# First two stacks of an attention kernel filled from tiles on chip, with the opening stage reordered

## The reference

```python
q, k, v = heads(x @ Wq + bq), heads(x @ Wk + bk), heads(x @ Wv + bv)      # x is layer-normalised
y  = softmax(causal(q @ k.T * scale)) @ v
qc, kc, vc = heads(x @ Wcq + bcq), heads(ctx @ Wck + bck), heads(ctx @ Wcv + bcv)
y += softmax(qc @ kc.T * scale) @ vc
x1 = x + (y @ Wp + bp)
z  = layernorm(x1); scores = (tanh(z @ gate_w.T) + 1) / 2
vals, idx = top_k(scores.T, 512)             # 4096 tokens, 8 experts
out = x1 + z.at[idx].add(expert_ffn(layernorm(z[idx])) * vals)
```

## Time and profile before

| | |
|---|---|
| median of three runs | 1717.27 us (1709.55 to 1719.33) |
| the profiled execution | 1720.7 us, of which the span is 1718.9 us |
| PE busy in the span | 1523.8 us (89%), mean granted clock 0.934 |
| DVE, ACT, POOL busy | 1176.9, 920.3, 427.0 us |

### The profile page before, as it was taken

The page is one execution under the profiler, slowest core; times in us unless marked ns, Lnnn a source line. Parts: engine busy times, 40 slices in busy tenths (PEclk is TensorE's granted clock), DMA queues, the critical chain, the costliest instruction groups (busy, mean ns, idle before and its releaser), DMA issues. The chain is left out here.

```text
span 1718.9 us, 26455 instructions
## 1 busy us (share of the span) xinstructions
PE 1523.8 (89%) x8913; PEld 719.2 (42%) x8913; DVE 1176.9 (68%) x3228; ACT 920.3 (54%) x1882; POOL 427.0 (25%) x863
## 2 busy tenths in 40 slices
PE   4469999999999999999999999999999624999997
PEld 3133344344434444443444344344433412566564
DVE  3367888788788778877887888787882156555441
ACT  2006777766677676777677677767767300211111
POOL 5002113132113213221321133131213301343332
PEclk9559999999999899999999999999999855999998
DMA  4981575285546727652855567185500120344332
GB/s 141 154 118 39 95 129 77 77 120 107 100 90 121 113 78 105 123 98 82 113 112 107 95 117 120 57 121 97 85 2 3 38 78 13 86 109 114 99 94 51
DMA packets 83467, 158.08 MB, mean 92 GB/s; under 512 B 12708, under 2 KB 46116, under 8 KB 83332
## 3 DMA queue, kind: packets, MB, share of 16 engines
q1 hardware_dynamic: 77188, 147.87, 44.8%
q0 software_dynamic: 6144, 8.52, 2.8%
HBM read 100.45 MB, written 55.71 MB: 91 GB/s over the span
## 5 line engine op out<-in xcount | busy, mean ns | idle before, releaser
L743 ACT ACTIVATE probs<-bank_ps 128x512 f32<-128x512 f32 (+3 forms) x1536 | 743.1, 545 | 297.6 <-PE bank_ps L541 291.9
L828 DVE TENSOR_REDUCE chunk_max<-bank_ps 128x1 f32<-128x512 f32 x1024 | 647.2, 682 | 112.3 <-PE bank_ps L572 109.8
L572 PE MATMUL bank_ps<-k_stack,q_stack 62*128 62x512 f32 (+3 forms) x1536 | 563.5, 446 | 32.5 <-DMA k_stack<-parts_dram 24.5
L541 PE MATMUL bank_ps<-q_stack,k_stack 64*128 64x512 f32 (+3 forms) x1536 | 545.5, 435 | 46.1 <-ACT probs L743 26.8
L572 PEld LDWEIGHTS bank_ps<-k_stack,q_stack 62*128 62x128 f32 x1536 | 256.0, 192 | 417.9 <-DVE chunk_max L828 180.3
L541 PEld LDWEIGHTS bank_ps<-q_stack,k_stack 64*128 64x128 f32 x1536 | 238.3, 188 | 133.2 <-ACT probs L743 103.9
L557 PE MATMUL out_ps<-probs,v_cross 128*32 128x512 f32 x2048 | 275.4, 610 | 0.0
L831 DVE CUSTOM_DVE_ANT_0 masked<-bank_ps,causal 128x128 bf16<-128x128 f32 (+3 forms) x512 | 232.3, 485 | 31.9 <-PE bank_ps L572 28.9
L986 POOL TENSOR_TENSOR pool_idle<-pool_idle 128x1 f32<-128x1 f32 x288 | 55.6, 193 | 627.9 <-ACT probs L743 429.5
L1263 ACT ACTIVATE h<-h_ps,b1T 128x512 f32<-128x512 f32 x64 | 44.0, 687 | 266.9 <-PE h_ps L1216 155.6
L887 DVE SCALAR_TENSOR_TENSOR parts<-bank_ps,bias,parts 128x512 fp32r<-128x512 f32 x80 | 60.0, 750 | 109.4 <-ACT parts L781 109.1
(11 more groups left out here) (147 smaller groups left out, 1313.5 us busy)
## 6 DMA issues: line engine op xcount, KB each, us to landing
parts_dram<-parts SPq DMA_DIRECT2D x80, 512.0 KB, 2.7
k_stack<-parts_dram SPq DMA_DIRECT2D x192, 192.0 KB, 11.7
q_stack<-parts_dram SPq DMA_DIRECT2D x192, 128.0 KB, 10.6
w1T<-in_L_ffn_fc1s SPq DMA_DIRECT2D x8, 1024.0 KB, 5.5
w2T<-in_L_ffn_fc2s SPq DMA_DIRECT2D x8, 1024.0 KB, 7.4
...
```

The costliest lines, as they stand in the source:

```text
L541: pe.matmul(bank_of(turn)[:, q0:T], k_stack[base:base + SIDE, g, pair, kc:kc + P], q_stack[base:base + SIDE, g, pair, qc + q0:qc + T], sta ...
L572: return pe.matmul(bank[:, 0:n], q_stack[base:base + MAX_ROWS, g, pair, qc:qc + P], k_stack[base:base + MAX_ROWS, g, pair, k0:k0 + n], sta ...
L743: nc.scalar.activation(probs[:, i % 2 * 2 + p, side, q0:T], bank_of(("score", g, i, p, side))[:, q0:T], ACT.Exp, scale=SCALE)\
L828: nc.vector.tensor_reduce(dst, bank[:, 0:n], AX.X, ALU.max).then_inc(max_done, 1)
```

## The change

- **Fills.** The stacks of units 0 and 1 are no longer read back from DRAM: `fill_directly` copies 16 rows of `parts` into 16 rows of a stack by DMA, one head at a time, so 24 DMAs a unit and half the size each. All 12 query copies of unit 0 go first, after qc is done; the 12 key copies after kc1; unit 1 follows. The first 24 maxima wait for one pair of heads (`first_in[0]`), the next 24 for the other, unit 1's for `second_in`.
- **Pieces.** The five pieces of half 1 move ahead of the value pieces and all maxima, and go to `probs` and `u_sb`, free at this time; their stores to DRAM follow the direct fills on SP. The three value pieces of half 0 run beside the maxima; those of half 1 move into the first batch, at (0, 1), (0, 4) and (0, 5), as in every other batch.
- **Opening.** Loads are split into what the first projections need (8) and the rest (7), with the context between them; x of sequence 1 is loaded after the first shift. DVE clears a quarter of `q_stack`, takes the statistics, and normalises x itself; POOL clears a quarter of `k_stack` first, makes the deviation, and clears the rest and the value tiles after it. Four matmuls on `ones_row` (`WARM_UP`) come first on PE.
- **Waits.** `fill` waits for one half fewer; ACT waits for the stores of half 1 before the first batch.

The core of the diff:

```diff
         return not (first and g == 0)
-    if name in LATER or (name in V_PIECES and half == 1):
+    if name in LATER:
         return not first
+    if name in V_PIECES and half == 1:
+        return True
...
-PROLOGUE = (("y0T0", 0), ("y0T1", 0), *((n, 0) for n in HALF_PIECES),
-            *((n, 0) for n in V_PIECES),
-            *((n, 1) for n in V_PIECES), *((n, 1) for n in HALF_PIECES), ("shift", 0))
-ALONE = PROLOGUE.index(("qc", 1))
+PROLOGUE = (("y0T0", 0), ("y0T1", 0), *((n, 0) for n in HALF_PIECES), *((n, 1) for n in HALF_PIECES),
+            *((n, 0) for n in V_PIECES), ("shift", 0))
+ALONE = PROLOGUE.index(("v", 0))
 UNWEIGHTED = 2
+WARM_UP = 4
...
+        def parts_of(piece):
...
+            if piece.of == 0 and piece.half == 1:
+                n = HALF_PIECES.index(piece.name)
+                return probs[:, n].bitcast(F32R) if n < 4 else u_sb[:].bitcast(F32R)
+            a, e = COL[piece.name]
+            return parts[:, :, a:e]
...
             def load_weights():
-                for name, tile in (("Wq", w_q), ("Wcq", w_cq), ("Wk", w_k), ("Wv", w_v), ("Wp", w_p)):
+                for name, tile in (("Wq", w_q), ("Wcq", w_cq), ("Wk", w_k)):
                     sp.dma_start(tile[:], w[name].rearrange("(t p) c -> p t c", p=P)).then_inc(weights_in, 16)
-                for name, tile in (("Wck", w_ck), ("Wcv", w_cv)):
-                    sp.dma_start(tile[:], w[name]).then_inc(weights_in, 16)
+                sp.dma_start(w_ck[:], w["Wck"]).then_inc(weights_in, 16)
...
                                  allow_slow_non_contiguous=True).then_inc(weights_in, 16)
...
+            def load_rest():
+                for name, tile in (("Wv", w_v), ("Wp", w_p)):
+                    sp.dma_start(tile[:], w[name].rearrange("(t p) c -> p t c", p=P)).then_inc(rest_in, 16)
+                sp.dma_start(w_cv[:], w["Wcv"]).then_inc(rest_in, 16)
...
                     sp.dma_start(bias_v[:, n, :], w[name].rearrange("(t p) -> p t", p=P),
-                                 allow_slow_non_contiguous=True).then_inc(weights_in, 16)
+                                 allow_slow_non_contiguous=True).then_inc(rest_in, 16)
                 sp.dma_start(bias_p[:], w["bp"].rearrange("(o c) -> o c", o=1).broadcast_to([P, C]))\
-                    .then_inc(weights_in, 16)
-                sp.dma_start(gateT[:], w["gate_w"].rearrange("p (t e) -> p t e", t=KT)).then_inc(weights_in, 16)
+                    .then_inc(rest_in, 16)
+                sp.dma_start(gateT[:], w["gate_w"].rearrange("p (t e) -> p t e", t=KT)).then_inc(rest_in, 16)
...
                 sp.wait_ge(*freed(piece))
-                if stacked is not None and name == HALF_PIECES[0]:
+                if stacked and name == HALF_PIECES[0]:
...
                         sp.wait_ge(slot_in[slot], stacked)
-                sp.dma_start(parts_dram[hf, :, :, a:e].rearrange("t c n -> c t n"), parts[:, :, a:e].bitcast(F32))\
+                sp.dma_start(parts_dram[hf, :, :, a:e].rearrange("t c n -> c t n"), parts_of(piece).bitcast(F32))\
...
                 hf, at = slot // 2, slot % 2 * UH * D
-                sp.wait_ge(parts_out, PARTS * halves)
+                sp.wait_ge(parts_out, PARTS * (halves - 1))
...
+            def fill_directly(slot, pair, of_q, landed):
...
+                a, e = (0, Q_COLS) if of_q else (Q_COLS, Q_COLS + K_COLS)
+                stack = q_stack if of_q else k_stack
+                for r, part in enumerate(Q_PART if of_q else K_PART):
+                    for side in range(SIDES):
+                        at = D * (UH * slot + SIDES * pair + side)
+                        to = SIDE * side + D * r
+                        sp.dma_start(stack[to:to + D, slot, pair].bitcast(F32), parts[at:at + D, part, a:e].bitcast(F32))\
+                            .then_inc(landed, 16)
...
                     for name in names:
-                        store_parts(find_piece(b, first, last, name, hf), FILL * b + FILL)
+                        store_parts(find_piece(b, first, last, name, hf), FILL * (b + hf))
...
                 if not last:
-                    sp.wait_ge(*freed(find_piece(b, first, last, "vc1", 1) if not first
-                                      else prologue_piece(PROLOGUE.index(("kc1", 1)))))
+                    sp.wait_ge(*freed(find_piece(b, first, last, "vc1", 1)))
...
             load_tokens(0)
+            load_weights()
             load_context(0)
-            load_weights()
-            sp.wait_ge(*freed(prologue_piece(PROLOGUE.index(("y0T1", 0)))))
-            load_tokens(1)
-            sp.wait_ge(stacks_clear, 2)
+            load_rest()
+            sp.wait_ge(q_clear, 3)
+            sp.wait_ge(k_clear, 2)
+            sp.wait_ge(*freed(prologue_piece(PROLOGUE.index(("qc", 0)))))
+            for pair in range(UH // SIDES):
+                fill_directly(0, pair, True, first_in[pair])
+            sp.wait_ge(*freed(prologue_piece(PROLOGUE.index(("kc1", 0)))))
+            for pair in range(UH // SIDES):
+                fill_directly(0, pair, False, first_in[pair])
+            for pair in range(UH // SIDES):
+                fill_directly(1, pair, True, second_in)
+                fill_directly(1, pair, False, second_in)
+            for name in HALF_PIECES:
+                store_parts(prologue_piece(PROLOGUE.index((name, 1))))
...
                                  [SHIFT_ROWS, UNITS * UH // SIDES * K_COLS // T, T])).then_inc(ones_in, 16)
-            for hf in range(2):
-                for name in HALF_PIECES:
-                    store_parts(prologue_piece(PROLOGUE.index((name, hf))))
-                fill(2 * hf, hf + 1)
-                fill(2 * hf + 1, hf + 1)
             put_shift(0, 0)
+            sp.wait_ge(*freed(prologue_piece(PROLOGUE.index(("y0T1", 0)))))
+            load_tokens(1)
+            fill(2, 2)
+            fill(3, 2)
...
                 kind, h, qt, chunk = MAX_ORDER[a]
-                if a == 0:
-                    pe.wait_ge(slot_in[g], FILL * b + FILL)
+                if b == 0 and g == 0:
+                    if a % (N_A // 2) == 0:
+                        pe.wait_ge(first_in[a // (N_A // 2)], DIRECT)
+                elif b == 0 and g == 1:
+                    if a == 0:
+                        pe.wait_ge(second_in, DIRECT * UH // SIDES)
+                elif a == 0:
+                    pe.wait_ge(slot_in[g], FILL * (b + g // 2))
...
-            def prologue_freed():
-                pe.wait_ge(*freed(prologue_piece(PROLOGUE.index(("vc1", 1)))))
-                pe.wait_ge(*freed(prologue_piece(max(n for n in range(len(PROLOGUE) - 1) if n < ALONE
-                                                     and PROLOGUE[n][0] in COL))))
...
+            pe.wait_ge(ones_set, 1)
+            for n in range(WARM_UP):
+                pe.matmul(bank_ps[:, BANKS - 1], ones_row[:, 0:P], ones_row[:], start=True, stop=True)
...
                 piece(prologue_piece(n), prologue_bank(n))
-            prologue_freed()
+            pe.wait_ge(rest_in, REST)
+            pe.wait_ge(*freed(prologue_piece(ALONE - 1)))
...
                 elif name in COL:
-                    a, e = COL[name]
                     halves = 2 * piece.of + hf
-                    if halves > 0:
-                        act.wait_ge(parts_out, PARTS * halves)
-                    nc.scalar.activation(parts[:, 0, a:e], bank[:], ACT.Identity,
+                    if halves > 2:
+                        act.wait_ge(parts_out, PARTS * (halves - 1))
+                    nc.scalar.activation(parts_of(piece)[:, 0], bank[:], ACT.Identity,
...
                 if n == UNWEIGHTED:
+                    act.wait_ge(weights_in, LOADS)
+                elif n == ALONE:
...
                 piece(prologue_piece(n), prologue_bank(n))
+            act.wait_ge(parts_out, PARTS)
...
-            nc.vector.memset(q_stack[:].bitcast(F32), 0.0).then_inc(stacks_clear, 1)
+            nc.vector.memset(ones_row[:], 1.0).then_inc(ones_set, 1)
+            nc.vector.memset(q_stack[:, 0].bitcast(F32), 0.0).then_inc(q_clear, 1)
...
             norm_stats(0, lambda t: x_sb[:, t, :], 1)
...
-            nc.vector.memset(ones_row[:], 1.0).then_inc(ones_set, 1)
+            nc.vector.memset(q_stack[:, 1].bitcast(F32), 0.0).then_inc(q_clear, 1)
+            dve.wait_ge(rstd_step[0], 2)
+            for t in range(NT):
+                nz = nc.vector.tensor_scalar(x_sb[:, t, :], x_sb[:, t, :], mean_var[:, 0, t, 0:1], rstd[:, 0, t:t + 1],
+                                             ALU.subtract, ALU.mult)
+            nz.then_inc(ln_done[0], 1)
+            nc.vector.memset(q_stack[:, 2:4].bitcast(F32), 0.0).then_inc(q_clear, 1)
             dve.wait_ge(weights_in, LOADS)
-            nc.vector.tensor_tensor(bias_v[:, 2, :], bias_v[:, 0, :], bias_v[:, 1, :], ALU.add).then_inc(v_bias_done, 1)
...
                 piece(prologue_piece(n), prologue_bank(n))
+            dve.wait_ge(rest_in, REST)
```

(6 more changed lines are left out.)

19 lines of the change are left out of this document (11 added, 8 removed).

## The result

The changed kernel takes 1689.24 us in the median of 4 runs (1687.51 to 1691.11), beside 1715.92 us (1709.55 to 1719.33) for the kernel before on the same chip: a ratio of 0.985, with 0.982 to 0.988 as its 95% interval. Timed a second time beside the experiments it took 1686.03 us (1684.95 to 1687.08), beside 1720.54: 0.981 (0.978 to 0.984). So it is faster by 1.5 to 1.9%. The prediction was 1687, with a range of 1671 to 1700. The medians lie 26.7 us apart, the two profiled executions that the stages are read from 33.2 us (1720.7 and 1687.5): of the four timed executions of the changed kernel the profiled one is the fastest, and that of the kernel before is slower than all four beside it.

What follows compares the result with a forecast made beforehand. PE was taken to bound the kernel from 150 us on, waits and DVE the opening. First maximum -21.5, unit 0's maxima -2.7, shift -12.7, first batch +6.8 sum to -30.1: 1717.3 to 1687 us, eight in ten 1671 to 1700.

Steps and rivals of the forecast that it cites:

- x ready at 17.85: Opening: POOL's k_stack clear holds DVE's normalising from 8.5 to 16.3 us, so x comes level with the 17.83 before.
- Rival B: Opening: POOL's v_self and v_cross clears get in between if engines take turns; x 5.3 us later, 1692 us; chance 0.17.
- x to the first copy: Opening: transposes and pieces keep their times, so qc's low half ends and SP can start copies at 27.6 us.
- Copies at 111 GB/s: Fills: SBUF-to-SBUF copies run at the old fills' rate; first pair's 1.38 MB takes 12.4 us, first maximum at 41.4.
- Unit 0's maxima 33.6 us: 27.6 us for maxima plus 6.0 for three value pieces beside them; 2.7 us less than before, done at 75.0.
- The shift, row maxima to first scores 12.2 us: Shift's store no longer behind queued fills; row maxima to first scores falls from 24.9 to 12.2 us, -12.7.
- The bound that was 0.6 us off deciding: SP's queue, at worst, lets scores start by 86.6 us; DVE's chain gives 87.2, later by only 0.6.
- First scores -36.9: End of the opening: first scores start at 87.2 us instead of 124.11.
- First batch +6.8: Three value pieces at 1.95 us on a full PE add 5.8 us, plus 1.0 for the first at half clock.
- The rest unchanged: After the opening: the same batches follow, fills and sequence 1's x land in time, ACT's new wait is met.
- Warm-up: Opening: four matmuls on idle PE cost nothing and, followed by some 8 idle us, bring nothing.
- rival A: Opening: no lock between clear and DVE; x ready at 10.0, PE warm, everything 10.5 us earlier, 1677 us; chance 0.2.

Runs made afterwards that it cites:

- the first pair first: Changed kernel with queries and keys of the first pair of heads copied before those of the second; 1677.41 us once, then 1683.66 us median.
- the values in the gap: Changed kernel with half 1's three value pieces moved from the first batch to between the projections and the first maximum; 1676.09 us.
- the last combination: Changed kernel with large GpSimd clears after normalisation, first pair's copies first, six warm-up matmuls, half 1's value pieces before the maxima; 1663.6 us once, then 1665.85 us median.

## Why the prediction was right, and where it was wrong

The result lies 2 us from the forecast and is faster by well over 0.5%, as 93 in 100 of the chances had it. But the sum was right partly because misses cancelled, which is luck: the first maximum came 5.1 us later than forecast, the maxima, the shift and the first batch together cost 10.6 us less, and 2.6 us were lost in the feed-forward part. By the profiled executions the gain is thus 33.1 us instead of 30.1, by the medians 26.7; the forecast lies between the two.

**x ready at 17.85: wrong, by 4.4 us.** The step said that the clear of `k_stack` holds VectorE's first instruction to its end. That mechanism is shown by the 7.43 us row of the kernel with one clear beside it. What failed is the step's silent assumption that VectorE goes next: GpSimd's two following clears came first too. Rival B had the size (5.3 us later) but thought of taking turns; in fact VectorE's instruction ended only when GpSimd's queue of clears was empty (21.33 against 21.17), and not between two of them. The Trainium skill ("SBUF — State Buffer", section "Who interferes with whom") says that the loser is fully blocked for the winner's whole instruction. The trace agrees, 7.43 us, and goes beyond it: the loser stayed blocked over three successive instructions, 12.62 us.

**x to the first copy: 9.75 us assumed, 10.3 measured** (22.29 to qc's low half done at 32.58). That is the rest of the 5.1 us by which the first maximum came late.

**Copies at 111 GB/s, bound by bytes: wrong in kind, right in size.** From the first copy to the first maximum the step gave 13.8 us, and 13.8 was measured (32.69 to 46.48). But the bound is the issue: 18 issues of 0.635 us are 11.4 us, and the last lands some 2.3 us later. 96 KB every 0.635 us are 155 GB/s, more than the rate taken. The step used SP's 0.46 us an issue of the earlier trace rows, and put the bound by issue 3.4 us earlier; the copies from SBUF cost 0.635. The agreement is a coincidence, and it would mislead wherever the count of copies changes and the bytes do not. Moving six query copies back does not tell the two apart by its gain (0.39 MB or 3.5 us by bytes, 3.8 by issue, 3.9 measured), but the steady 2.7 to 2.9 us from issue to landing does.

**Unit 0's maxima 33.6 us: 30.3 measured.** The mis-sized term is the value pieces beside them, set at 6.0 us from half-clock rows. Over the 27.6 us that the step gave to the maxima alone it was 2.7 here, 6.1 in the repeat of the changed kernel, and 1.1 with the first pair first (28.7 us, at full clock up to 56 us). It depends on the clock, which is not the same from run to run with the same code. Busy time by stretch, first of the changed kernel, then of its repeat:

```profile
50.00:54.00 4.00, 3.28 (x21) 2.22 (x19) 2.71 (x8) 1.17 (x2) 0.00 (x0) 0.98 0.77 121
```

```profile
50.00:54.00 4.00, 3.64 (x14) 2.56 (x13) 2.30 (x7) 0.58 (x1) 0.00 (x0) 0.50 0.82 125
```

At granted clock 0.50 from 46 to 62 us the repeat took 33.7 us for these maxima, nearly the predicted figure; the first profiled execution was back at full clock by 50 us and took 30.3.

**The shift, row maxima to first scores 12.2 us: right,** 11.4 measured, with no wait for the read-back. The kernel with the shift behind the fills shows that the queue's order did it. The bound that was 0.6 us off deciding did not decide: SP's queue was empty enough at 77.95 for the store to go at once.

**First scores -36.9: right,** -35.9 measured. The late first maximum (+5.1), quicker maxima (-3.3) and a quicker shift (-0.8) nearly cancel.

**First batch +6.8: wrong, +0.3 measured** (23.42 before, 23.71 after, from first scores to unit 1's row maxima). The step took 1.95 us for each of three pieces "on a PE that has no room", and rested this on the earlier trace rows for 150 to 200 us. The first batch's beginning is not that stretch. With the values in the gap this part takes 21.8 us in two kernels, so the three pieces cost some 1.9 us and not 5.8. The other 1.6 us go with the clock, and two executions of one kernel show its price. Both are of the last combination, without the pieces, from the first scores to unit 1's row maxima; first the one timed once, then its repeat:

```profile
70.40:92.20 21.80, 20.41 (x106) 7.92 (x106) 18.18 (x49) 14.79 (x28) 6.46 (x8) 0.83 1.03 128
```

```profile
70.30:93.60 23.30, 22.29 (x106) 8.51 (x106) 18.31 (x49) 14.80 (x28) 6.46 (x8) 0.74 1.03 143
```

The same 106 matmuls take 1.5 us longer at a mean granted clock of 0.74 than at 0.83. The kernel before, which has no pieces here either, took 23.42 us at 0.73; the changed one, with them, 23.71 at 0.87. So the clock was back sooner in the changed kernel, and that hid most of what the pieces cost.

**The rest unchanged: nearly.** The covered loads, the move of x of sequence 1 and ACT's new wait cost nothing that shows: the 35.7 us stand from the eighth unit to the feed-forward part. That part then takes 339.6 us instead of 337.0. In the experiments it took 339 to 342 us; why it was 337.0 in the one trace of before stays open.

**Warm-up: right,** no effect. The prediction's rival A gave it 2.7 us if x came at 10. With x at 9.83 four matmuls did not bring that, since they ended 1.95 us too early (q 3.75 us); with six, transposes and q took 3.0 us instead of 5.7, which is those 2.7 us.
